# A graph attention kernel: the softmax shift broadcast by two matmuls 256 columns wide instead of four 128 wide

## The reference

```
h   = relu(layernorm(x));  x = x + GAT(h);  h = relu(layernorm(x));  x = x + GCN(h)

one attention pass (heads H, width C):
  h    = (x @ W).reshape(N, H, C)
  al_s = sum_c h * a_src ;  al_d = sum_c h * a_dst          # one score per node and head
  e    = leaky_relu(al_s[src] + al_d[dst], 0.2)
  m    = segment_max(e, dst)
  ex   = exp(e - m[dst]);   alpha = ex / (segment_sum(ex, dst)[dst] + 1e-16)
  out  = segment_sum(h[src] * alpha, dst) + bias
```

## Time and profile before

| | before |
|---|---|
| median of 3 runs | 1183.21 us |
| the profiled execution's own time | 1184.0 us |
| its span, first to last instruction | 1181.9 us |
| PE busy, matmuls | 1115.0 us, 94% |
| DVE busy | 839.9 us, 71% |
| ACT busy | 513.1 us, 43% |
| POOL busy | 53.9 us, 5% |
| mean granted TensorE clock | 0.987 |

### The profile page before, as it was taken

One profiled execution on the slowest core, in us unless ns is written; L12 is line 12 of the kernel. 1 busy time (PEld: TensorE's weight loads), 2 busy tenths in 40 slices (PEclk: granted clock), 3 DMA queues, 4 the chain that ended last, 5 costly groups with the idle time before them and its releaser, 6 DMA issues. The chain is left out here.

```text
span 1181.9 us, 17595 instructions
## 1 busy us (share of the span) xinstructions
PE 1115.0 (94%) x7126; PEld 1045.1 (88%) x7126; DVE 839.9 (71%) x1394; ACT 513.1 (43%) x1052; POOL 53.9 (5%) x50
## 2 busy tenths in 40 slices
PE   5999999989999999999999999958999899999998
PEld 5878886789989998999989999848999899889998
DVE  7998895889759887689767778889856633341263
ACT  4232322275546654555546754235535613431120
POOL 4200001020000000000000000340000000000000
PEclk9999999999999999999999999979999999999999
DMA  6133130021011100201011100022002200000321
GB/s 221 62 118 116 38 125 18 1 63 54 1 36 55 54 1 1 90 1 55 1 47 43 55 1 1 2 94 77 28 27 82 103 1 1 27 14 1 131 76 55
DMA packets 27618, 58.44 MB, mean 49 GB/s; under 512 B 3492, under 2 KB 6152, under 8 KB 27536
## 3 DMA queue, kind: packets, MB, share of 16 engines
q1 hardware_dynamic: 27344, 56.96, 14.2%
q10 hardware_dynamic: 192, 0.32, 0.1%
HBM read 41.73 MB, written 15.54 MB: 48 GB/s over the span
## 5 line engine op out<-in xcount | busy, mean ns | idle before, releaser
L1442 PE MATMUL banks<-hs,ring_hi 128*128 128x258 f32 (+1 forms) x1600 | 297.9, 287 | 4.3 <-DVE z L1047 4.3
L1442 PEld LDWEIGHTS banks<-hs,ring_hi 128*128 128x128 f32 (+1 forms) x1600 | 246.7, 188 | 5.7 <-DVE z L1047 4.5
L1442 PE MATMUL banks<-hs,ring_lo 128*128 128x258 f32 (+1 forms) x800 | 226.1, 283 | 0.0
L247 ACT ACTIVATE e<-banks,al 128x256 f32<-128x256 f32 (+1 forms) x500 | 193.9, 491 | 28.9 <-PE banks L232 28.9
L255 ACT ACTIVATE ring_hi<-pf 128x512 fp32r<-128x512 f32 (+1 forms) x125 | 81.6, 653 | 160.3 <-DVE pf L266 157.1
L1442 PEld LDWEIGHTS banks<-hs,ring_lo 128*128 128x128 f32 (+1 forms) x800 | 150.1, 188 | 0.0
L1470 PE MATMUL banks<-w_hi,oT_hi 128*128 128x384 f32 (+1 forms) x320 | 110.3, 345 | 11.6 <-DVE rows L1075 7.2
L1470 PE MATMUL banks<-w_hi,oT_lo 128*128 128x384 f32 (+1 forms) x320 | 109.6, 343 | 0.0
L264 DVE TENSOR_TENSOR e<-e 128x512 f32<-128x512 f32 (+1 forms) x125 | 84.6, 676 | 35.0 <-ACT e L247 34.5
L1470 PE MATMUL banks<-w_lo,oT_hi 128*128 128x384 f32 (+1 forms) x320 | 109.4, 342 | 0.0
L1316 PE MATMUL banks<-w_hi,xT_hi 128*128 128x512 f32 x240 | 98.3, 409 | 0.3 <-DVE w_lo L829 0.3
(11 more groups left out here) (265 smaller groups left out, 2135.6 us busy)
## 6 DMA issues: line engine op xcount, KB each, us to landing
h_scratch<-stage SPq DMA_DIRECT2D x30, 256.0 KB, 2.0
hs<-h_scratch SPq DMA_DIRECT2D x30, 256.0 KB, 2.9
w_st<-in_L_gnn_W SPq DMA_DIRECT2D x4, 1536.0 KB, 7.3
w_st<-in_L_gnn_W SPq DMA_DIRECT2D x16, 384.0 KB, 3.3
gw_st<-in_L_gnn_W SPq DMA_DIRECT2D x12, 384.0 KB, 4.0
xr<-in_x SPq DMA_DIRECT2D x9, 384.0 KB, 10.1
rows<-in_x SPq DMA_DIRECT2D x9, 384.0 KB, 6.1
x_scratch<-rows SPq DMA_DIRECT2D x9, 384.0 KB
```

The costliest lines, as they stand in the source:

```text
L247: last = nc.scalar.activation(self.e[:, local % 2, a, i, 0:n], self.p_shift[:, a, 0:n], ACT.Exp, bias=scores[a][:, g * G + i:g * G + i + 1])
L1442: last = nc.tensor.matmul(p_a[0:m, dt, half, 0:HH], wt.ring[a][:, s // G, s % G, dt * P:dt * P + m], hs[:, s, b, half * HH:(half + 1) * HH ...
```

## The change

A broadcast is now two matmuls, one for each a, with 256 columns. Its weights are the 40 x 2 table of_part (ones in all rows of part a), made once by DVE. Its moving operand is a new table spread, 40 rows of 2 x 128: in half dt it holds the shift rows of tile c*NDT+dt in these rows' own places and zeros elsewhere. That is made by multiplying all 40 rows with one column of own_tile (40 x 10, ones where a row belongs to the tile), twice per chunk.

spread is made by DVE straight from the turned shifts in PSUM where a new shiftT comes (`spread_from`, for a head's first chunk, for SECOND and SECOND+1), and by ACT from shiftT for each other chunk (`spread_rows`), behind hi of the last group of the chunk before. PE waits for the new semaphore spread_done before these broadcasts. shiftT has three places instead of four.

```
     def broadcast(self, nc, pe, mem, q):
 
         pe.wait_ge(self.e_ready, q * NG + 1)
         for a in range(2):
-            for dt in range(NDT):
-                row = a * T + c * NDT + dt
-                last = nc.tensor.matmul(self.p_shift[:, a, dt * P:(dt + 1) * P],
-                                        pick[:, row:row + 1].to_broadcast([4 * T, P]), shift_rows,
-                                        start=True, stop=True)
+            last = nc.tensor.matmul(self.p_shift[:, a, :], mem.of_part[:, a:a + 1].to_broadcast([4 * T, P]),
+                                    mem.spread[:, :, :].rearrange("r t c -> r (t c)"), start=True, stop=True)
         last.then_inc(self.shift_in, 1)
...
+def spread_from(nc, mem, p_shift, c, done):
+    for dt in range(NDT):
+        t = c * NDT + dt
+        last = nc.vector.tensor_scalar(mem.spread[:, dt, :], p_shift, mem.own_tile[:, t:t + 1], None, ALU.mult)
+    last.then_inc(done, 1)
+
+def spread_rows(nc, act, mem, slot, c, done):
+    for dt in range(NDT):
+        t = c * NDT + dt
+        last = nc.scalar.activation(mem.spread[:, dt, :], mem.shiftT[:, slot, :].bitcast(fp32), ACT.Copy, scale=mem.own_tile[:, t:t + 1])
+    last.then_inc(done, 1)
...
             nc.gpsimd.tensor_tensor(mem.own_tile[:, :], pick[:, 0:T].bitcast(fp32), pick[:, T:2 * T].bitcast(fp32), ALU.add).then_inc(made, 1)
...  ACT, chunk q of head h
                     wt.hi(nc, act, q, c, NG - 1)
                     if c == 0:
                         split_rows(h, 4)
+                    if c + 1 < NC:
+                        act.wait_ge(shift_out, h + 1)
+                        spread_rows(nc, act, mem, h % 2, c + 1, spread_done)
                     if c == 1:
                         split_weights(h, range(2, KH))
...  DVE, once
+            def part_rows():
+                nc.vector.tensor_reduce(mem.of_part[:, :], pick[:, :].bitcast(fp32).rearrange("r (a t) -> r a t", a=2), AX.X, ALU.max).then_inc(of_part_ready, 1)
...  DVE, once per head
             def keep_shift(h):
                 dve.wait_ge(shift_t, h + 2)
-                nc.vector.tensor_copy(shiftT[:, h + 1, :], p_g[1][0:4 * T, 0:P]).then_inc(shift_out, 1)
+                nc.vector.tensor_copy(shiftT[:, (h + 1) % 2, :], p_g[1][0:4 * T, 0:P])
+                dve.wait_ge(wt.shift_in, (h + 1) * NC)
+                spread_from(nc, mem, p_g[1][0:4 * T, 0:P], 0, shift_out)
...  PE, sums(q) of head h
                     if s == G - 1 and c + 1 < NC:
-                        wt.broadcast(nc, pe, pick, shiftT[:, h, :], q + 1, c + 1)
+                        pe.wait_ge(spread_done, h * (NC - 1) + c + 1)
+                        wt.broadcast(nc, pe, mem, q + 1)
...  ACT, second layer, chunk c
             wt.hi(nc, act, SECOND + c, c, NG - 1)
+            if c + 1 < NC:
+                spread_rows(nc, act, mem, 1, c + 1, spread_done)
...  PE, second layer
                 if s == G - 1 and 1 <= c < NC - 1:
-                    wt.broadcast(nc, pe, pick, shiftT[:, 2, :], SECOND + c + 1, c + 1)
+                    pe.wait_ge(spread_done, HEADS * (NC - 1) + c)
+                    wt.broadcast(nc, pe, mem, SECOND + c + 1)
```

More of the change, by code:

```diff
@@ L100, in __init__ @@
         self.al02 = own("al02", [P, T, NV], fp32)
-        self.shiftT = own("shiftT", [4 * T, HEADS, P], f32r)
+        self.shiftT = own("shiftT", [4 * T, 3, P], f32r)
+        self.spread = own("spread", [4 * T, NDT, P], f32r)
+        self.own_tile = own("own_tile", [4 * T, T], fp32)
+        self.of_part = own("of_part", [4 * T, 2], f32r)
         self.vcol = own("vcol", [P, KD, NV], fp32)
@@ L383, in first_layer @@
     picked = sem("picked")
+    of_part_ready, spread_done = sem("of_part_ready"), sem("spread_done")
     red_ready = sem("red_ready")
@@ L431, in first_layer @@
     p_shift_first, p_shift_rest = banks[0:4 * T, 6, 2 * P:3 * P], banks[0:4 * T, 6, 3 * P:4 * P]
-    half = second_half(nc, st, mem, *later, tile_in, banks, wt, g_ready, scored)
+    half = second_half(nc, st, mem, *later, tile_in, banks, wt, g_ready, scored, spread_done)
     hs2, hi2_done, lo2_done = half.hs, half.hi_done, half.lo_done
@@ L536, in _ @@
                 pool_.wait_ge(made, 13 + r)
+            nc.gpsimd.tensor_tensor(mem.own_tile[:, :], pick[:, 0:T].bitcast(fp32), pick[:, T:2 * T].bitcast(fp32), ALU.add).then_inc(made, 1)
             nc.gpsimd.iota(codes[:, :, :, :], pattern=[[OFFSET, 2], [0, FIX], [1, WK]], base=0, channel_multiplier=0).then_inc(made, 1)
             nc.gpsimd.iota(place[:, :], pattern=[[1, NCH]], base=0, channel_multiplier=0).then_inc(made, 1)
-            pool_.wait_ge(made, 16)
+            pool_.wait_ge(made, 17)
             for i, (t0, t1) in enumerate(PARTS):
@@ L938, in _ @@
             edge_keys()
+            part_rows()
             ahead = 0
@@ L1014, in _ @@
             dve.wait_ge(shift_t, 1)
-            nc.vector.tensor_copy(shiftT[:, 0, :], p_s0).then_inc(shift_out, 1)
+            nc.vector.tensor_copy(shiftT[:, 0, :], p_s0)
+            dve.wait_ge(made, 17)
+            spread_from(nc, mem, p_s0, 0, shift_out)
             degree_sums(range(1, 5))
@@ L1228, in _ @@
             dve.wait_ge(shift_t, HEADS + 1)
-            nc.vector.tensor_copy(shiftT[:, 0, :], p_shift_first).then_inc(shift_out, 1)
+            dve.wait_ge(wt.shift_in, SECOND)
+            spread_from(nc, mem, p_shift_first, 0, shift_out)
             second_top(8, REST_COLS)
@@ L1253, in _ @@
             dve.wait_ge(shift_t, HEADS + 2)
-            nc.vector.tensor_copy(shiftT[:, 2, :], p_shift_rest).then_inc(shift_out, 1)
+            nc.vector.tensor_copy(shiftT[:, 1, :], p_shift_rest)
+            dve.wait_ge(wt.shift_in, SECOND + 1)
+            spread_from(nc, mem, p_shift_rest, 1, shift_out)
             wt.weigh(nc, dve, counts, SECOND, 0, 4)
@@ L1391, in spread_first @@
             def spread_first():
+                pe.wait_ge(of_part_ready, 1)
                 pe.wait_ge(shift_out, 1)
-                wt.broadcast(nc, pe, pick, shiftT[:, 0, :], 0, 0)
+                wt.broadcast(nc, pe, mem, 0)
             between = {0: score_columns, 4: turn_top, 5: lambda: turn_shift(0, p_s0), 6: spread_first, 9: degrees}
@@ L1447, in sums @@
                     if s == G - 1 and c + 1 < NC:
-                        wt.broadcast(nc, pe, pick, shiftT[:, h, :], q + 1, c + 1)
+                        pe.wait_ge(spread_done, h * (NC - 1) + c + 1)
+                        wt.broadcast(nc, pe, mem, q + 1)
                     if s == 2 * G - 1 and c == NC - 1 and not final:
                         pe.wait_ge(shift_out, h + 2)
-                        wt.broadcast(nc, pe, pick, shiftT[:, h + 1, :], q + 1, 0)
+                        wt.broadcast(nc, pe, mem, q + 1)
                     if c == NC - 2 and not final:
@@ L1490, in _ @@
             pe.wait_ge(shift_out, HEADS + 1)
-            wt.broadcast(nc, pe, pick, shiftT[:, 0, :], SECOND, 0)
+            wt.broadcast(nc, pe, mem, SECOND)
             def turn_rest():
@@ L1502, in spread_rest @@
                 pe.wait_ge(shift_out, HEADS + 2)
-                wt.broadcast(nc, pe, pick, shiftT[:, 2, :], SECOND + 1, 1)
+                wt.broadcast(nc, pe, mem, SECOND + 1)
             half.tensor(pe, {1: turn_rest, 5: lambda: turn_shift(HEADS + 1, p_shift_rest), 6: spread_rest})
@@ L1528, with second_half @@
     pass
-def second_half(nc, st, mem, x, b2, G1, c1, G2, c2, x2_scratch, out, tile_in, banks, wt, g_ready, scored):
+def second_half(nc, st, mem, x, b2, G1, c1, G2, c2, x2_scratch, out, tile_in, banks, wt, g_ready, scored, spread_done):
     pb, sem = makers(nc, st)
@@ L1849, in vector @@
                 dve.wait_ge(turned, 1)
-                nc.vector.tensor_copy(shiftT[:, 1, :], p_turn).then_inc(turn_out, 1)
+                nc.vector.tensor_copy(shiftT[:, 2, :], p_turn).then_inc(turn_out, 1)
         def row_lo(t):
@@ L1974, in spread_roots @@
                 last = nc.tensor.matmul(p_wide[:, (t - t0) * P:(t - t0 + 1) * P], pick[:, t:t + 1].to_broadcast([4 * T, P]),
-                                        shiftT[:, 1, :], start=True, stop=True)
+                                        shiftT[:, 2, :], start=True, stop=True)
             last.then_inc(wide_ready, 1)
```

2 lines of the change are left out of this document (1 added, 1 removed).

## The result

The changed kernel takes 1233.02 us, median of 4 runs (1231.77 to 1237.37), where the kernel before took 1182.35 (1180.92 to 1185.86); the ratio is 1.0421 with a 95% interval of 1.0397 to 1.0444. The forecast was 1217, its range ended at 1228: slower as expected, by half as much again as expected, and outside the range. The profiled execution took 1237.37 us with a span of 1235.2, so it lies 4.4 us above its own median. The traces are compared span with span, 53.3 us apart; the medians are 50.7 apart.

The account below looks back on a forecast made before the run. PE, busy 94% of the span, was taken to bound the kernel. Waits +34.9, clock +3.2 and matmuls -4.6 gave +33.5 us on the profiled 1184.0, less 0.8 to the median: about 1217 us, range 1198 to 1228.

Parts of the forecast that it names:

- When the table is ready: Broadcasts of c=0 to 3: the table is never ready in time; PE starts 0.6 us after ring_hi's end.
- The lateness repeats: Attention chunks: ring_hi is tied to PE through DVE, so a slipping PE drags it along and waits in each chunk.
- Rival 1: DVE and ACT work on while PE stands, so half the waiting is given back; 1196 us, chance 0.16.
- rival 2: PE slips once by head 0's 5.9 us, later tables are early, so not slower; 1179.5 us, chance 0.06.
- Price of a wait without its clock: New waits at the broadcasts, priced head by head less what older waits swallow; part of the +34.9 us for waits.
- Clock elsewhere, +3.2 (0 to 8): Behind c=1 waits of heads 1 to 3: cold restarts of 1.6 us each, two counted, +3.2 us.
- Rival 3: Cold restarts also behind c=0's 2.6 us waits, and head 0's shifts stack up; +8, 1225 us, chance 0.12 with rival 4.
- rival 4: At the broadcast, the wide matmul costs twice the narrow one; +4.6, 1222 us, chance 0.12 with Rival 3.
- The matmuls, -4.6: Each broadcast takes 0.39 us instead of 0.59, since weights set a narrow matmul's pace; 23 times 0.2 is -4.6 us.
- DVE's extra instructions, +0.45 a head: At c=4, two more DVE instructions come before the semaphore that products wait for; +0.45 us per head.

Follow-up runs that it names:

- the filled kernel: The changed kernel, with PE running extra 256-wide matmuls that are overwritten while it waits for the table; 1216.5 us, ratio 1.0263 to the kernel before.
- The wait alone: The kernel before, with PE only waiting for the chunk's last ring_hi ahead of 19 broadcasts, no table; 1213.79 us, ratio 1.0257.

## Why the prediction was wrong, by its own steps

- **When the table is ready: right.** PE waits for ACT's spread at c=0 to 3, 0.64 us behind the last ring_hi (0.6 forecast), 1.68 in c=0 where the two hs lie between. 38.1 us in 18 waits against some 40 in 19; moving the pair alone takes all of it away. Single waits were off: 4.9 in the first chunk of head 0 against 6.5, 3.1 in c=1 of head 3 against 4.3.
- **The lateness repeats: right.** Waits of c=1 were 4.5 us in heads 1 and 2, 4.3 forecast, and the lateness grows by 14.2 us in either. Rival 1 (half given back) and rival 2 (one slip) fell with this, and the waits that were to absorb some of it did: 5.9 us in all.
- **Price of a wait without its clock: right as far as can be seen.** From q=5 to q=9 the filled kernel, which has no low stretch there, loses 6.9 us (10.31 to 17.20); the forecast had 7.3 for these waits, less some 0.8 for the matmuls. The wait alone is no test of it: its 7.3 us hold the clock as well.
- **Clock elsewhere, +3.2 (0 to 8): the step that failed.** Two restarts were priced in head 0 as well, 3.2 us; but before's own restart at 262.99 drops out there, since the forecast runs sums(1) at full clock, so the clock was to cost 4.8 us over before. It cost some 23 in the profiled executions: 23.4 by PE's busy time, or 20.2 that the fills took away and the 3 that they left; by the medians the fills took away 16.5, which makes it some 19. Two things were wrong. The step gave a cold restart only to waits over 4 us, since the one restart looked up followed 4.3 us, but the clock also fell behind the 2.6 us waits of c=0 and the 1.7 us waits of c=2, and behind the products' 2.0. The trace of before could have told: its low stretches at 499.05 and 632.16 begin 1.0 and 1.5 us after waits of 1.93 us:

```profile
498.06 0.41 PE L1470 MATMUL banks<-w_hi,oT_hi 128*128 128x384 f32 x1 [1.93 <-DVE rows L1075]
...
630.68 0.41 PE L1470 MATMUL banks<-w_hi,oT_hi 128*128 128x384 f32 x1 [1.93 <-DVE rows L1075]
```

  And each restart was priced as one low stretch of 3.4 us. The 1.6 us for that was right (1.5 by the pace above), but behind the 4.5 us waits of c=1 and the 2.6 us waits of c=0 in heads 2 and 3 it lasted 6.8 us, and at the 5.8 us wait of head 0 10.2 us (from 273.06 on, within the wait that ended at 276.58). Rival 3 had the first of these, at +8 where 15 to 19 were missing, and shared its chance of 0.12 with rival 4: too little for a size that no row bounded from above.
- **The matmuls, -4.6: right.** 0.43 us instead of 0.39 for a broadcast, 4.0 instead of 4.6 for all. Four narrow matmuls do not cost what two of twice the width cost (0.59 against 0.43), so the columns alone do not set their pace; rival 4 is excluded. That the weights set it was the prediction's reading of the 0.107 us; no run varied the weights alone.
- **DVE's extra instructions, +0.45 a head: right in the wait, not in its consequence.** The wait grew by 0.5 per head (4.4 to 6.0). In the filled kernel a low stretch stood behind it in all three heads, in the changed one in two, in before (waits of 1.5) in none; where it stood, the step cost 1.8 to 1.9 us instead of 0.45.

The sum for the profiled executions: waits 38.1, less 5.9 absorbed, plus DVE's 2.6 (products 1.6, rows 0.7, the broadcast fed by DVE 0.3), less 4.0 for the matmuls, is 30.8; with the clock's 23.4 it comes to 54.2, against 53.3 measured. The share of each wait in the clock's part is not settled, since only all fills together were run.

The last ring_hi of q=0 ends 1.8 us sooner than in before (250.5, not 252.3). The traces explain 1.5 of it: the low stretch at 198.67 is in before alone, and PE is 1.5 us ahead of it from there on. All the kernels that were run afterwards, and the changed one, have a low stretch at 241 to 243.5 us instead. PE had no wait of over 0.25 us in the 7 us ahead of either, but issued twenty small matmuls, of 8 columns in the first place and of one in the second; why the clock fell there is open.

## What to carry to other kernels

The new wait on PE, which bounds this kernel, has to be priced twice, once in idle time and once in the granted clock of the work behind it; here the second came to 23 of 53 us. The price of the clock is not read from one restart: list every low stretch of the trace with the wait ahead of it, take every new wait as long as the shortest of these (1.9 us here) for a likely restart, and bound the sum by more than one low stretch for each. And a small result that the next stage waits for belongs ahead of the slow step in its engine's queue: waiting for the same instructions cost 4.2% behind the last ring_hi and nothing measurable ahead of it.

## What the runs showed of the hardware that was not expected

- TensorE's granted clock fell from 1.00 to 0.50 behind waits as short as 1.7 us (c=2 of heads 0 to 2). The length of the wait alone does not tell whether and for how long: the 1.93 us waits for rows had a low stretch behind them in two of three heads of before and in none of the changed kernel; waits of 2.6 us (c=0) were followed by 3.4 us at the lower level in head 1 and by 6.8 in heads 2 and 3, those of 4.5 us (c=1, heads 1 and 2) by 6.8, that of 3.1 us in head 3 by 3.4.
- At the lower level the 258-wide matmuls start 0.65/3 = 0.22 us apart, at full clock 0.12: such time is lost by 45%.
- Matmuls whose result nobody uses, put where PE stands, went with a granted clock of 1.00 (416.50 to 419.90) where the changed kernel has 0.50 (421.40 to 424.80) and were worth 16.5 us of 1233.
- The same kernel's runs spread with the clock they were granted. Of 23 runs of the kernel before on one chip the fastest had a span of 1177.6 us at 0.987, the slowest 1185.6 at 0.983. A difference of this size between two single executions says little about the kernels.
